# A slot-attention and mixture-of-experts kernel: all engines' calls in another planned order up to the first tile of expert work

## The chip, the core and the metric

The kernel runs on one NeuronCore of one Trainium2 chip. The time is the device time of one execution in microseconds (us), the median of three runs. All arithmetic is in fp32. The names of the engines are those of the profile: PE is TensorE's matmul and PEld its weight load, DVE is VectorE, ACT is ScalarE, POOL is GpSimd, SP is SyncE, which here issues transfers only.

## The reference, cut to what matters

The input x has 2 batches of 1024 tokens with 256 features. Each token is refined by three rounds of attention over a small context (154 rows a batch) and by a small MLP; then each token goes to 8 of 32 experts, beside one shared expert.

```python
k, v = x_in @ wk + bk, x_in @ wv + bv              # x_in: normalised context
slots = q_mu + exp(q_logsig) * layernorm(x)        # one slot per token
for _ in range(3):
    q = ln(slots) @ wq + bq
    attn = softmax(k q^T / scale, over the slots) + 1e-8   # so a softmax spans all 1024 tokens
    slots = (attn / attn.sum(over context)) v @ wu + bu + slots
    slots = gelu(ln(slots) @ w1 + b1) @ w2 + b2 + slots
    slots = ln(slots + cond)
x = x + slots
h = layernorm(x)
scores = sigmoid(h @ gate_w.T)                     # 32 experts, 8 chosen in 4 of 8 groups
combine = 2.5 * scores[chosen] / sum
out = x + sum_e combine_e * (silu(h gate_e) * (h up_e)) down_e + shared(h)
```

## The kernel before, in words

The 2048 tokens are four blocks of 512: blocks 0 and 1 are the first batch, 2 and 3 the second. The program has two parts.

**The front.** Each block passes three rounds. In one round r, a block i goes through these calls, each of which is a helper function on one engine with the same name in the engines' programs: `square` (ACT, L1394) and `from_squares` (POOL, L545 to L540) give the variance and rstd of the slots, `normalise` (ACT, L1402) writes them, `transpose_slots` (PE, L1649) turns them, `evacuate` (ACT, L1409) copies them out of PSUM, and `logits` (PE, L1663) multiplies with the keys. `maxima` (DVE, L771) and `exponent_bias` (DVE, L781, L787), one for both blocks of a batch, `exponent` (ACT, L1419) and `scale_values` (DVE, L794 to L803) make the softmax. `attend` (PE L1678, DVE L811 to L765) comes in two halves a block; the second half on PE waits until DVE has read the banks of the first. Then square, from_squares, normalise, transpose and evacuate again, `hidden` (PE L1689), `gelu` (ACT L1429), `project_back` (PE L1702), `condition` (POOL L568 or DVE L822, which adds the condition row to 512 tokens), `residual` (DVE L831), `slot_moments` (DVE L733 to L739), `from_moments` (POOL L536) and `norm_slots` (DVE L743, L749). A softmax needs both blocks of its batch, so a batch's blocks go in step; the two batches are independent of each other.

After round 2 a block is routed: `add_tokens` (DVE L840 and moments), `from_tokens` (POOL L559), `normalise` into tokrow (ACT L1402), `transpose_block`, `copy_tokens` (ACT L1436), `gate_logits` (PE L1714), `score_tokens` (ACT L1440), `choose` (DVE L855 to L891: the 8 experts), `weigh` (DVE L896 to L909), `rank` (PE L1723 to L1729: at which place of its expert each token goes) and `find_places` (DVE L920 to L930). POOL's `dispatch` (L609) then scatters the block's 512 token rows to DRAM with 32 indirect DMAs, two in each of 16 steps. It waits for placed and weighed of its block. Beside this run the shared expert (`shared_gate_up` PE L1781 and L1787, `shared_silu` ACT L1446, `shared_product` DVE L1020, `shared_down` PE L1798, `add_shared` DVE L1028) and the tables of which expert each tile has (`count_runs` PE L1744, `tabulate_runs`, `tabulate_steps`, `tabulate_tiles` DVE, `sum_runs` and `spread_runs` PE), in three phases. The first phase needs blocks 0 and 1, the last one all blocks.

**The tiles.** 159 tiles of 128 token rows follow. SP fetches a tile, PE turns it (L1886), multiplies with its expert's weights (L2027), turns the activation (L2040) and multiplies down (L2047); ACT writes the weighted result (`copy_out`, L1477). POOL scatters 153 of these results to DRAM (`scatter`, L704), each when its result is there. After dispatch step 12 of block 2, POOL issues one scatter after each dispatch step, until the dispatches of blocks 2 and 3 are all out. At the end SP fetches the results in token order, DVE adds them, and SP stores them. `turn_act(0)`, the first L2040, waits until all four blocks' shared results are added.

**What sets the order.** Each engine works through its queue strictly in program order and waits at semaphores. The order of the front is a plain list of calls written out by hand or by a planner in each engine's program, and this list is all that the change touches. A call that waits holds back everything behind it on its engine, on POOL the dispatches too. From the first tile on the order is that of loops.

## Time and profile before

| | us |
|---|---|
| median of 3 runs | 616.68 (615.47 to 618.01) |
| profiled execution, span | 615.6 |
| median less span | 1.1 |
| PE busy | 563.7 (92%) |
| POOL busy | 363.9 (59%) |
| first dispatch starts | 212.26 |
| first turn of an activation (L2040) starts | 336.40 |
| last scatter starts | 590.54 |

The span is from the first to the last instruction on the core; no other time of the profiled execution is given. Issuing an indirect DMA counts as busy on POOL, the 0.3 us between two of them do not, so POOL's 59% understates how full its queue is.

### The profile page before, as it was taken

Reading aid. Unit: us, or ns where it says so; the run is one execution under the profiler, and the core shown is the slowest. Engines: PE = TensorE matmul, PEld = TensorE weight load, DVE = VectorE, ACT = ScalarE, POOL = GpSimd, SP = SyncE. Lnnn points to the kernel's source line nnn. Section 1 sums busy time; section 2 is a strip of 40 time slices with the busy share of each in tenths; the row PEclk is TensorE's granted clock in tenths of the full one; section 3 lists DMA queues with packets and bytes.
Section 4 is the critical chain, followed back from the end, with each engine's and each line's share of the span. In section 5 each row is a group of like instructions: output and inputs, shape, how many; then the busy total and the mean of one; then the engine's idle time right before and its main releaser. Section 6 shows DMA issues by size and latency. Waiting matters only on the chain.

```text
span 615.6 us, 11543 instructions
## 1 busy us (share of the span) xinstructions
PE 563.7 (92%) x2669; PEld 419.9 (68%) x2669; DVE 411.4 (67%) x1587; ACT 372.2 (60%) x993; POOL 363.9 (59%) x414
## 2 busy tenths in 40 slices
PE   3989989889998898698998999999999999999995
PEld 2656557655766455455656888888888888888774
DVE  6965675986768987648776444445444444698778
ACT  1858888768776755552611666566566666676660
POOL 4334233622143377886777777777777777777730
PEclk9979999999999799899799999999999999999998
DMA  7999300000000023239364999876666667999956
GB/s 259 394 397 380 120 0 2 0 1 0 2 0 1 14 94 118 97 118 341 119 223 179 314 315 338 284 224 205 202 207 201 210 199 216 353 412 397 413 184 244
DMA packets 62063, 119.69 MB, mean 194 GB/s; under 512 B 8667, under 2 KB 45583, under 8 KB 59951
## 3 DMA queue, kind: packets, MB, share of 16 engines
q1 hardware_dynamic: 48079, 77.63, 37.5%
q0 software_dynamic: 13488, 41.04, 17.7%
q8 instruction: 25, 0.41, 0.3%
q10 hardware_dynamic: 432, 0.29, 0.2%
q14 instruction: 39, 0.32, 0.2%
HBM read 61.29 MB, written 57.64 MB: 193 GB/s over the span
## 4 chain that ended last, share of the span: by engine, by line
PE 70%; DVE 10%; POOL 6%; ACT 6%; DMA 5%; issue 3%; SPq 0%; DVEq 0%; POOLq 0%; ACTq 0%
PE ps L2027 20%; PE ps L2047 10%; PE ps L1689 6%; PE ps L1663 6%; PE ps L1678 5%; PE ps L1886 5%; PE ps L1702 5%; POOL xrows L609 4%; DMA hat<-yrows 3%; PE ps L2040 3%; PE ps L1649 2%; PE ps L1781 2%; PE ps L1787 2%; DVE tokrow L749 2%; DMA xs<-in_x 1%
## 5 line engine op out<-in xcount | busy, mean ns | idle before, releaser
L2027 PE MATMUL ps<-arena,mats 128*128 x636 | 164.2, 381 | 0.3 <-issue 0.3
L609 POOL DMA_INDIRECT xrows<-tokrow,place_of x128 | 125.8, 983 | 42.9 <-issue 37.2
L1274 DVE TENSOR_TENSOR mats<-ps,mats 128x128 f32<-128x128 f32 x159 | 46.3, 291 | 104.1 <-ACT mats L1460 99.8
L2027 PEld LDWEIGHTS ps<-arena,mats 128*128 128x128 f32 x636 | 108.5, 190 | 9.3 <-issue 0.8
L2047 PE MATMUL ps<-arena,mats 128*128 x318 | 95.7, 383 | 1.0 <-DVE mats L1281 1.0
L1460 ACT ACTIVATE mats<-ps 128x128 f32<-128x128 f32 x159 | 44.1, 277 | 57.0 <-PE ps L2027 57.0
L1453 ACT COPY mats<-ps 128x256 f32<-128x256 f32 x159 | 57.9, 364 | 11.8 <-PE ps L1886 11.8
L1402 ACT ACTIVATE hat<-tokrow,shift,rstd 128x256 f32<-128x256 f32 x96 | 49.7, 590 | 14.1 <-POOL shift L540 14.1
L1394 ACT ACTIVATE hat<-tokrow,total 128x256 f32<-128x256 f32 x96 | 47.5, 499 | 17.0 <-DVE tokrow L814 10.3
L2047 PEld LDWEIGHTS ps<-arena,mats 128*128 128x128 f32 x318 | 48.0, 191 | 13.5 <-issue 1.9
L545 POOL TENSOR_SCALAR var_eps<-variance 128x4 f32<-128x4 f32 x24 | 6.4, 266 | 83.5 <-ACT hat L1394 83.2
L704 POOL DMA_INDIRECT yrows<-hatT,mats x48 | 46.4, 967 | 14.6 <-issue 10.4
L1689 PE MATMUL ps<-hatT,arena 128*128 128x512 f32 x96 | 48.6, 654 | 4.4 <-ACT hatT L1409 4.4
L1702 PE MATMUL ps<-mats,hat 128*128 128x256 f32 x192 | 44.4, 384 | 4.5 <-ACT hat L1429 4.5
L1663 PE MATMUL ps<-hatT,arena 128*128 128x512 f32 x96 | 44.8, 615 | 2.1 <-ACT hatT L1409 2.1
L2040 PE MATMUL ps<-ident,mats 128*128 128x128 f32 x159 | 43.6, 274 | 2.7 <-DVE mats L1274 2.5
L704 POOL DMA_INDIRECT yrows<-tokrow,mats x38 | 38.5, 1013 | 11.6 <-issue 9.4
L1702 PEld LDWEIGHTS ps<-mats,hat 128*128 128x128 f32 x192 | 35.6, 190 | 13.7 <-ACT hat L1429 4.8
L1678 PE MATMUL ps<-arena 128*128 128x257 f32 x192 | 44.3, 384 | 0.1
L1678 PEld LDWEIGHTS ps<-arena 128*128 128x128 f32 x192 | 36.1, 192 | 6.8 <-DVE arena L803 1.2
L1689 PEld LDWEIGHTS ps<-hatT,arena 128*128 128x128 f32 x96 | 19.8, 211 | 27.1 <-issue 21.2
L536 POOL TENSOR_TENSOR rstd<-var_eps,minus_half 128x4 f32<-128x4 f32 x16 | 18.6, 1165 | 29.1 <-DVE var_eps L739 29.0
(239 smaller groups left out, 1136.4 us busy)
## 6 DMA issues: line engine op xcount, KB each, us to landing
hat<-xrows SPq DMA_DIRECT2D x81, 160.0 KB
rows<-xrows SPq DMA_DIRECT2D x78, 160.0 KB
arena<-in_experts SPq DMA_DIRECT2D x4, 1920.0 KB, 18.9
xrows<-padrow SPq DMA_DIRECT2D x32, 160.0 KB
hat<-yrows SPq DMA_DIRECT2D x5, 1024.0 KB, 9.0
tokrow<-yrows SPq DMA_DIRECT2D x5, 1024.0 KB, 9.6
hatT<-yrows SPq DMA_DIRECT2D x5, 1024.0 KB, 9.3
xrows<-padrow SPq DMA_DIRECT2D x1, 4960.0 KB
```

Source lines behind the costliest of these rows:

```text
L609: gp.indirect_dma_start(out=xrows[:, :], out_offset=bass.IndirectOffsetOnAxis(ap=place_of[:, g, k:k + 1], axis=0), in_=tokrow[:, g, :], in ...
L704: gp.indirect_dma_start(out=yrows[:, :], out_offset=bass.IndirectOffsetOnAxis(ap=scatter_to[:, n:n + 1], axis=0), in_=ybuf[y_place(n)], in ...
L1394: it = ac.activation(hat[:, g, :], slots[:, g, :], ACT.Square, bias=total[:, g:g + 1], scale=-float(D), accum_out=variance[:, g:g + 1])
L1402: ac.activation(into[:, g, :], source[:, g, :], ACT.Identity, bias=shift[:, g:g + 1], scale=rstd[:, g:g + 1]).then_inc(normed[i // Q], 1)
L1453: ac.copy(turned_row[u], bank(4 + u)[:, 0:D]).then_inc(row_copied, 1)
L1663: mm = te.matmul(bank(banks_of(i)[h]), kq[:, dc, j * NH:j * NH + P], hatT[b][:, dc, span_of(i)], start=dc == 0, stop=dc == DC - 1)
L1678: mm = te.matmul(bank(banks_of(i)[k])[:, 0:D + 1], attn[b][:, h, t * P:(t + 1) * P], vscaled[b][:, h, 0:D + 1], start=h == 0, stop=h == 1)
L1689: mm = te.matmul(bank(banks_of(i)[fc]), w1g[:, dc, fc * P:(fc + 1) * P], hatT[b][:, dc, span_of(i)], start=dc == 0, stop=dc == DC - 1)
L1702: mm = te.matmul(bank(banks_of(i)[k])[:, t * D:(t + 1) * D], gel[i][:, fc, s:s + P], mat("w2", fc), start=fc == 0, stop=fc == DC - 1)
L2027: mm = te.matmul(bank(6 + u)[:, 0:2 * I], turned_row[u][:, dc * P:(dc + 1) * P], arena[:, dc * D:(E - 1) * WCOL + (dc + 1) * D][:, bass.ds ...
L2040: te.transpose(bank(u)[:, 0:I], act[u], ident[:, :]).then_inc(act_turned, 1)
L2047: te.matmul(bank(2 + u)[:, 0:D], actT[u], arena[:, 2 * D:(E - 1) * WCOL + 3 * D][:, bass.ds(at, D)], start=True, stop=True).then_inc(down_ ...
```

## The change

Four lists of calls have another order: those of POOL, DVE, ACT and PE, from the start to the first tile. No call is added, removed or altered, and SP's program is the same. On the whole the calls of the second batch's attention stand later among those of the first batch; `constants` and `run_constants` move, and in the last stage the shared expert's calls and the counts stand elsewhere. The core of the diff, PE first, then DVE and POOL:

```diff
             attend(0, 2, 1)
+            transpose_slots(3, 2)
             attend(1, 2, 1)
+            logits(3, 1)
+            transpose_slots(0, 5)
+            transpose_slots(1, 5)
+            hidden(0, 2)
             attend(2, 1, 0)
-            attend(3, 1, 0)
-            attend(2, 1, 1)
-            transpose_slots(0, 5)
-            attend(3, 1, 1)
-            hidden(0, 2)
-            transpose_slots(1, 5)
             project_back(0, 2)
             hidden(1, 2)
+            project_back(1, 2)
+            attend(2, 1, 1)
+            attend(3, 1, 0)
             transpose_slots(2, 3)
-            project_back(1, 2)
+            attend(3, 1, 1)
+            transpose_block(0, 2 * ROUNDS, slots)
+            gate_logits(0)
             hidden(2, 1)
             project_back(2, 1)
+            rank(0)
             transpose_slots(3, 3)
-            transpose_block(0, 2 * ROUNDS, slots)
-            gate_logits(0)
             hidden(3, 1)
-            rank(0)
...
+            spread_runs(0)
             project_back(2, 2)
-            shared_gate_up(1, 0)
             hidden(3, 2)
...
             sum_runs(1)
-            shared_gate_up(3, 1)
             spread_runs(1)
             count_runs(2)
+            shared_gate_up(3, 1)
+            sum_runs(2)
             shared_down(3)
...
             slot_moments(1)
+            attend(2, 1, 1)
             add_tokens(0)
-            residual(2, 1)
-            slot_moments(2)
-            norm_slots(2, 1)
+            attend(3, 1, 0)
+            norm_slots(1, 2)
+            attend(3, 1, 1)
+            add_tokens(1)
             choose(0)
             weigh(0)
             find_places(0)
...
             from_tokens(0)
             from_moments(1, 4)
-            from_moments(2, 3)
-            from_squares(2, 4)
+            from_squares(3, 3)
+            from_tokens(1)
             dispatch(0, 0)
             dispatch(0, 1)
+            from_moments(2, 3)
             dispatch(0, 2)
-            from_tokens(1)
             dispatch(0, 3)
+            from_squares(2, 4)
             from_moments(3, 3)
```

On PE, from the first batch's last project_back (the first L1702; mats is w2, hat is gelu's output) to rank(0) (L1723, whose input mats is the table of chosen experts). Before:

```order
L1702 MATMUL ps<-mats,hat 128x256 x8
L1689 MATMUL ps<-hatT,arena 128x512 x4
L1702 MATMUL ps<-mats,hat 128x256 x8
L1649 MATMUL ps<-ident,hat 128x128 x8
L1649 MATMUL ps<-ident,tokrow 128x128 x8
L1714 MATMUL ps<-gwT,hatT 128x32 x8
L1689 MATMUL ps<-hatT,arena 128x512 x4
L1723 MATMUL ps<-mats,routing 128x128
```

and in the changed program, the same stretch:

```order
L1702 MATMUL ps<-mats,hat 128x256 x8
L1678 MATMUL ps<-arena 128x257 x8
L1649 MATMUL ps<-ident,hat 128x128 x8
L1678 MATMUL ps<-arena 128x257 x4
L1649 MATMUL ps<-ident,tokrow 128x128 x8
L1714 MATMUL ps<-gwT,hatT 128x32 x8
L1689 MATMUL ps<-hatT,arena 128x512 x4
L1702 MATMUL ps<-mats,hat 128x256 x8
L1723 MATMUL ps<-mats,routing 128x128
```

Three halves of the second batch's attention (L1678) have come between the last project_back of the first batch and the gate, and the block that hidden and project_back (L1689, L1702) serve behind the gate is now block 2, both of them ahead of rank(0).

On POOL, from the last from_tokens ahead of the dispatches on (L559 is from_tokens, L609 the dispatches, L536 from_moments, L545 to L540 from_squares). Before:

```order
L559 TENSOR_TENSOR rstd<-var_eps,minus_half 128x4
L540 TENSOR_TENSOR shift<-neg_mean,rstd 128x4
L536 TENSOR_TENSOR rstd<-var_eps,minus_half 128x4 x2
L545 TENSOR_SCALAR var_eps<-variance 128x4
L548 TENSOR_TENSOR rstd<-var_eps,minus_half 128x4
L540 TENSOR_TENSOR shift<-neg_mean,rstd 128x4
L609 DMA xrows<-tokrow,place_of 73600x320 x6
L559 TENSOR_TENSOR rstd<-var_eps,minus_half 128x4
L540 TENSOR_TENSOR shift<-neg_mean,rstd 128x4
L609 DMA xrows<-tokrow,place_of 73600x320 x2
```

and in the changed program:

```order
L559 TENSOR_TENSOR rstd<-var_eps,minus_half 128x4
L540 TENSOR_TENSOR shift<-neg_mean,rstd 128x4
L609 DMA xrows<-tokrow,place_of 73600x320 x4
L536 TENSOR_TENSOR rstd<-var_eps,minus_half 128x4
L609 DMA xrows<-tokrow,place_of 73600x320 x4
L545 TENSOR_SCALAR var_eps<-variance 128x4
L548 TENSOR_TENSOR rstd<-var_eps,minus_half 128x4
L540 TENSOR_TENSOR shift<-neg_mean,rstd 128x4
L536 TENSOR_TENSOR rstd<-var_eps,minus_half 128x4
L609 DMA xrows<-tokrow,place_of 73600x320 x4
```

from_tokens(1) has moved ahead of the first dispatch, and from_moments(2, 3) and from_squares(2, 4), which stood ahead of it, now stand between the dispatches.

## Rows read from the trace of the kernel before

**Rows 1.** The chain that ended last, its end: start us, us, what

```profile
590.54 4.44 DMA yrows<-tokrow,mats
...
595.03 4.97 DMA hat<-yrows
```

**Rows 2.** POOL's timeline: start us, us, what, [idle before <-releaser]

```profile
212.26 1.21 POOL L609 DMA_INDIRECT xrows<-tokrow,place_of  x1 [5.40 <-DVE place_of L929]
...
221.36 1.04 POOL L559 TENSOR_TENSOR rstd<-var_eps,minus_half 128x4 f32<-128x4 f32 x1 [1.25 <-DVE var_eps L739]
...
283.72 1.04 POOL L536 TENSOR_TENSOR rstd<-var_eps,minus_half 128x4 f32<-128x4 f32 x1 [1.47 <-DVE var_eps L739]
...
288.44 1.20 POOL L559 TENSOR_TENSOR rstd<-var_eps,minus_half 128x4 f32<-128x4 f32 x1 [1.18 <-DVE var_eps L739]
...
311.94 0.96 POOL L609 DMA_INDIRECT xrows<-tokrow,place_of  x1 [0.30 <-issue]
```

**Rows 3.** The page's groups, the dispatches: count, busy us, mean ns, idle before

```profile
L609 POOL DMA_INDIRECT xrows<-tokrow,place_of x128 | 125.8, 983 | 42.9 <-issue 37.2
```

**Rows 4.** ACT's timeline, its write of the last scattered result

```profile
589.43 0.47 ACT L1477 ACTIVATE tokrow<-ps,mats 128x256 f32<-128x256 f32 x1
```

**Rows 5.** PE's timeline from the first batch's last attention on

```profile
158.02 12.30 PE L1678 MATMUL ps<-arena 128*128 128x257 f32 x56
...
172.77 3.60 PE L1689 MATMUL ps<-hatT,arena 128*128 128x512 f32 x8
...
177.14 3.72 PE L1702 MATMUL ps<-mats,hat 128*128 128x256 f32 x16
...
203.30 6.47 PE L1689 MATMUL ps<-hatT,arena 128*128 128x512 f32 x8 [1.33 <-ACT hatT L1409]
```

**Rows 6.** POOL's condition and DVE's exponent_bias beside it, and one by itself

```profile
59.18 4.66 POOL L568 TENSOR_TENSOR tokrow<-tokrow,rows 128x1024 f32<-128x1024 f32 x2
...
61.13 2.73 DVE L781 SCALAR_TENSOR_TENSOR shifted<-rowmax,qk_bias 77x1 f32<-77x1 f32 x2
...
95.37 0.35 DVE L781 SCALAR_TENSOR_TENSOR shifted<-rowmax,qk_bias 77x1 f32<-77x1 f32 x2
```

**Rows 7.** DVE's timeline, norm_slots(0, 2) to weigh(0)

```profile
184.76 1.66 DVE L743 SCALAR_TENSOR_TENSOR tokrow<-tokrow,mv,rows 128x256 f32<-128x256 f32 x4
...
187.97 0.68 DVE L831 TENSOR_TENSOR tokrow<-ps,tokrow 128x512 f32<-128x512 f32 x1
...
191.56 1.22 DVE L840 TENSOR_TENSOR xs<-xs,tokrow 128x1024 f32<-128x1024 f32 x1
...
195.11 0.69 DVE L831 TENSOR_TENSOR tokrow<-ps,tokrow 128x512 f32<-128x512 f32 x1 [0.20 <-PE ps L1702]
...
202.90 0.29 DVE L855 TENSOR_TENSOR mats<-mats,gbias 128x128 f32<-128x128 f32 x1
...
208.19 0.28 DVE L896 TENSOR_TENSOR mats<-mats 128x128 f32<-128x128 f32 x1
```

**Rows 8.** Two stretches: us, busy of PE, PEld, DVE, ACT, POOL; PEclk, DMA, GB/s

```profile
202.10:208.90 6.80, 5.60 (x7) 2.50 (x8) 6.22 (x45) 5.11 (x15) 1.41 (x3) 0.50 0.00 0
256.70:263.50 6.80, 5.79 (x11) 2.52 (x11) 2.42 (x3) 5.09 (x10) 5.78 (x7) 0.50 0.27 98
```

**Rows 9.** PE's timeline: logits(3, 2), transpose_slots(2, 5), last project_back, first L2040

```profile
234.30 3.70 PE L1663 MATMUL ps<-hatT,arena 128*128 128x512 f32 x8 [1.05 <-ACT hatT L1409]
...
255.86 2.17 PE L1649 MATMUL ps<-ident,hat 128*128 128x128 f32 x8 [3.63 <-ACT hat L1402]
...
277.06 3.72 PE L1702 MATMUL ps<-mats,hat 128*128 128x256 f32 x16 [0.78 <-ACT hat L1429]
...
336.40 0.33 PE L2040 MATMUL ps<-ident,mats 128*128 128x128 f32 x1 [0.96 <-DVE mats L1274]
```

**Rows 10.** DVE's timeline, the row behind choose(2), and tabulate_runs(2)

```profile
302.58 0.69 DVE L1020 TENSOR_TENSOR hat<-ps,hat 128x512 f32<-128x512 f32 x1
...
326.17 0.19 DVE L955 SCALAR_TENSOR_TENSOR pad_at<-ps,first_row 128x32 int32<-128x32 f32 x1 [2.02 <-PE ps L1744]
```

More of the change, by code:

```diff
@@ L625, in gpsimd_program @@
             condition(0, 0)
+            constants()
             condition(1, 0)
@@ L1130, in vector_program @@
             slot_moments(1)
+            norm_slots(1, 0)
             attend(2, 0, 0)
-            norm_slots(1, 0)
+            maxima(0, 1)
+            attend(3, 0, 0)
             attend(2, 0, 1)
-            attend(3, 0, 0)
-            maxima(0, 1)
+            attend(3, 0, 1)
             maxima(1, 1)
             exponent_bias(0, 1)
-            attend(3, 0, 1)
             scale_values(0, 1)
@@ L1184, in vector_program @@
             find_places(0)
-            run_constants()
-            norm_slots(1, 2)
+            condition(2, 1)
+            residual(2, 1)
+            slot_moments(2)
             condition(3, 1)
-            add_tokens(1)
+            norm_slots(2, 1)
             residual(3, 1)
@@ L1191, in vector_program @@
             norm_slots(3, 1)
-            shared_product(0, 0)
             choose(1)
@@ L1196, in vector_program @@
             exponent_bias(1, 2)
-            shared_product(0, 1)
+            shared_product(0, 0)
+            scale_values(1, 2)
             find_places(1)
-            scale_values(1, 2)
+            weigh(1)
+            attend(3, 2, 0)
+            attend(2, 2, 0)
+            attend(2, 2, 1)
+            attend(3, 2, 1)
             tabulate_runs(0)
-            attend(2, 2, 0)
             tabulate_steps(0)
-            attend(3, 2, 0)
-            attend(2, 2, 1)
-            tabulate_tiles(0)
-            attend(3, 2, 1)
-            weigh(1)
             condition(2, 2)
-            add_shared(0)
             residual(2, 2)
             slot_moments(2)
-            shared_product(1, 0)
+            tabulate_tiles(0)
             condition(3, 2)
+            shared_product(0, 1)
             norm_slots(2, 2)
@@ L1216, in vector_program @@
             slot_moments(3)
+            add_tokens(2)
+            add_shared(0)
+            shared_product(1, 0)
             shared_product(1, 1)
-            add_tokens(2)
             norm_slots(3, 2)
             add_tokens(3)
+            choose(2)
             add_shared(1)
-            choose(2)
             shared_product(2, 0)
```

188 lines of the change are left out of this document (90 added, 98 removed).

## The prediction, made before the changed kernel ran

> **What bounds the kernel now.** I read the end of the chain of waits first. The last scatter's transfer lands at 594.98, one fetch of 4.97 us and the last sums follow [rows 1]. So the end hangs on the last scatter, which is issued at 590.54. Then POOL's timeline, backwards: from the first dispatch at 212.26 [rows 2] it issues 128 dispatches and 153 scatters, and an issue costs 0.98 us and some 0.29 us between two (37.2 us over 126) [rows 3], so about 1.27 us. 281 of them are 356 us of the 378 us between 212.26 and 590.54; the other 22 us are small operations of the front that stand between the dispatches, and short waits. POOL's queue is thus full to the end. But the tiles finish beside it: ACT has written the last scattered result at 589.90 [rows 4], 0.64 us before its scatter, so only some 0.3 us of slack are left beyond the usual gap. So there are two clocks that have to be moved together: POOL's first dispatch with what stands between the dispatches, and PE's first tile. The later of the two sets the end. The last of the tables that the tiles read need the last round of the second batch, so the first tile hangs on the second batch's chain; the first dispatch hangs on the first batch's.
>
> **The stretch 150 to 215.** Before, PE does seven halves of attention in one piece, 12.30 us, 1.76 us each [rows 5]; the last of them are the second batch's, and they fill the time in which DVE, ACT and POOL carry the first batch from its attention to hidden(0, 2) at 172.77. The changed order puts these halves later and hides nothing in their place. I follow it with the durations of before.
> - Up to the first batch's last attention the shifts cancel within 1.5 us: the softmax of batch 0 no longer queues behind logits(2, 1) and (3, 1), and attend(0, 2, 0) starts 1.4 us earlier, after an idle PE of some 3 us. Hidden(0, 2) starts at about 171.8, 1.0 earlier.
> - Now gelu(0, 2) stands on ACT behind exponent(2, 1) and (3, 1), and those wait for logits(3, 1) (ends 168.6), maxima(3, 1) and exponent_bias(1, 1) (at 169.4). Just then POOL adds condition(0, 2) and (1, 2). Beside such a pair exponent_bias took 2.73 us and ended with POOL; alone it takes 0.35 [rows 6]. Held, the two exponents end at 176.7, gelu(0, 2) at 179.3, and project_back(0, 2) starts at 179.7 in place of 177.14 [rows 5]: 2.5 us late. Not held, it is 0.4 late.
> - By 3.60 and 3.72 us for hidden and project_back [rows 5], project_back(1, 2) then ends at 191.4 (held case). DVE: residual and moments to 194.2, attend(2, 1, 1) 1.4, add_tokens(0) 3.4 (191.56 to 195.11, less 0.2 of wait), attend(3, 1, 0) 1.4, norm_slots(1, 2) 3.3 (184.76 to 187.97) [rows 7], attend(3, 1, 1) 1.4, add_tokens(1) 3.4: choose(0) can start at 207.9, in place of 202.90.
> - PE has little in 191 to 206: three halves, of which the last waits for DVE until 200, two transposes, and the gate. Before, a thinner stretch of this kind, 197 to 203, ended with the clock granted at 0.50 for 6.8 us [rows 8], and hidden(3, 1) took 6.47 instead of 3.60 [rows 5], 2.9 us more. I take the same for hidden(2, 1): 206.2 to 212.7.
> - rank(0) stands behind it and project_back(2, 1): gelu, 3.72 us, rank 1.0, ends at 218.1. Choose(0) ends at 213.2 (5.29 us, 202.90 to 208.19) [rows 7] and weigh at 215.4, so it is rank that decides. With find_places 1.5 the first dispatch starts at 220.0: 7.7 late; at full clock 5.0.
>
> **From there to the end.** Two sums.
> - POOL: from the first dispatch to dispatch(2, 0) before 99.7 us (212.26 to 311.94) [rows 2]. Out goes from_tokens(1) with its 1.25 us wait, 2.7; in come from_moments(2, 3) 1.3 and from_squares(2, 4) 1.85; the waits of 1.47 and 1.18 [rows 2] go, since DVE and PE are ahead of the later queue there; two waits of 0.4 us come for from_squares(2, 5) and (3, 5). Together 2.2 us less. So dispatch(2, 0) is at 7.7 - 2.2 = 5.5 late. From it on the queue is the same.
> - PE: rank(0), hidden(3, 1) and project_back(3, 1) come in a row from 218.1, project_back(3, 1) also behind transpose_block(1) and ends at 230.5 (10 us late). Residual, moments, norm_slots(3, 1) (behind from_moments(3, 3), which waits for POOL's dispatches) and the same again for from_squares(3, 4) bring logits(3, 2) to 245.0, 10.7 after the 234.30 of before [rows 9]. From there 5 us come back: hidden(3, 2) follows project_back(2, 2) without the shared_gate_up(1, 0) of 3.6 us between, and I charge no half clock there (before, 6.8 us at 0.50 [rows 8] added some 2.4 to hidden(2, 2)); 0.8 is lost otherwise. The last project_back starts at 282.5, 5.4 after 277.06 [rows 9]. Choose(2) is then 7.8 late at 310.3 (302.5 before [rows 10]), since shared_product(1, 1) now waits in front of norm_slots(3, 2) (2.4). In the tables 1.4 comes back: count_runs(2) no longer stands behind shared_gate_up(3, 1), so DVE's wait of 2.02 [rows 10] goes, but shared_product(3, 1) and add_shared(3) still hold the end. First turned activation: 336.40 + 7.8 - 1.4 = 342.8, 6.4 late.
>
> The end follows the later: 6.4 less the 0.3 us of slack that results had to scatters, 6.1. Its lower bound is with both doubtful terms out: 2.1 (exponent_bias not held) and 2.9 (clock not dropped), 1.1. Its upper bound is a second drop of the clock in the thin stretch around 250 to 256, where before a drop followed at 256.7 [rows 8]: two halves at half speed, 3 us, so 9.1. Whether exponent_bias is held turns on tenths of a microsecond, so I count half of it: 6.1 - 1.1 = 5.0. The span would be 620.6, and with the 1.1 us by which the median stands above it, 621.7.
>
> Two rules of the Trainium skill bear on these two terms. "SBUF — State Buffer", section "SBUF: two separate sides", says that VectorE operations with two SBUF inputs and GpSimd exclude each other from a shared port pair for a whole instruction; the trace agrees with 2.73 us against 0.35 [rows 6]. By it alone the hold would count in full, and the time would be 622.8. "TensorE: Matmul & The Clock Gate", Part 1, says that an idle array falls to half rate and that activity releases it; the trace shows the same at 202.1 [rows 8]. It speaks against any order that leaves PE thin, and by it the half clock would count in full, as I have it.
>
> **Rivals.**
> 1. A wash. The doubtful terms fall away and the front's last stage gives more than I count: POOL's 2.2 us and the tables' 1.4 us are certain by order, and if rank(0) ends by 212 and choose(2) at its old place, both clocks shift by -1.4: 615.3. For it: a walk over 150 calls drifts, and mine has the early part even. Against: DVE alone puts choose(0) 3 to 5 us later. Range 614 to 619.
> 2. Faster. The place is the second batch's last round: before, PE waits 3.63 us ahead of transpose_slots(2, 5) [rows 9] and then runs at 0.50 until 263.5 [rows 8], 6 us together. If that hole closes and the first dispatch is not late, PE's first tile comes 6 us earlier, and POOL decides with its 2.2 us and what the first dispatch gains; with 2 us gained there, 4 us in all: 612.7. It needs the first dispatch before 213, from which point on it decides. Against: three of DVE's calls and two of PE's are newly ahead of it.
> 3. Much slower. POOL waits in its queue for the second batch (from_squares(2, 4), from_moments(3, 3), from_squares(3, 4), each with dispatches behind it), since that batch is 10 us late while the dispatches are 7.7: every microsecond of such a wait is one at the end. Three waits of 1.5 us and the second drop of the clock give 5.0 + 4.5 + 3 = 12: 629.
> 4. That nothing moves, because the end is set by something the order doesn't touch: excluded, since both clocks begin in the reordered part.
>
> **How the numbers follow.** My forecast, 617.8 to 625.8 (1.1 to 9.1 late), has 0.55; the wash 0.25; faster 0.14; much slower 0.06. 0.5% is 3.1 us, about what a measurement of this kernel can tell from no change: faster is below 613.6, slower above 619.8. Of my forecast a sixth lies below 619.8. Slower: 0.46 + 0.06, about 0.53; same: 0.09 + 0.22, 0.31; faster: 0.14 and a little of the wash, 0.16. The range for 8 in 10 is 613.0 to 627.0; the forecast's own is 617.8 to 625.8.
>
> **What would show it.** Of the changed kernel: POOL's first dispatch at 217 to 220 and dispatch(2, 0) 2 us less late than it; PE idle for 10 us or more between 186 and 206 and a clock of 0.50 behind that; rank(0), PE's first L1723, as late as the dispatch behind it; exponent_bias at about 170 with 2 us or more; logits(3, 2) 10 us late; the first L2040 at 341 to 343; the last scatter at 595 to 597. I am wrong if the first dispatch is before 214, or if DVE reaches choose(0) by 204.

## The result: 3.8% slower, 23 us where 5 were forecast, and the profile after

The changed kernel takes 639.4 us (median of 4 runs, 638.13 to 643.0) against 616.08 of the kernel before beside it (4 runs, 614.92 to 618.01): a ratio of 1.038, 95% interval 1.035 to 1.041. The sign was right and the size was not: 639.4 lies far above my range.

The end of the chain of waits of the changed kernel (start us, us, what), for [rows 1]:

```profile
615.68 2.77 DMA yrows<-tokrow,mats
...
618.50 4.88 DMA hat<-yrows
```

The last scatter is 25.1 us later than before. POOL's timeline, first dispatch and last scatter (in brackets the idle time before and what ended it), for [rows 2]:

```profile
224.59 2.06 POOL L609 DMA_INDIRECT xrows<-tokrow,place_of  x1 [9.26 <-DVE place_of L929]
...
615.68 1.32 POOL L704 DMA_INDIRECT yrows<-tokrow,mats  x1 [0.61 <-ACT tokrow L1477]
```

The first dispatch is 12.3 us late, but POOL's queue no longer decides: its last scatter waits 0.61 us for ACT. The tiles decide, and PE's first turned activation is at 363.02 in place of 336.40 [rows 9], 26.6 late; from it to the end of the span take 276.0 us in place of 279.2. So the question is where PE's 26.6 us arose. PE's account up to its first turned activation, of the kernel before (span of time, busy of PE, PEld, DVE, ACT, POOL with counts, mean granted clock, DMA share, GB/s):

```profile
0.00:336.40 336.40, 293.95 (x1205) 194.34 (x1205) 249.15 (x1013) 205.31 (x478) 168.84 (x217) 0.96 0.36 129
```

and of the changed kernel:

```profile
0.00:363.02 363.02, 304.16 (x1205) 202.57 (x1205) 248.30 (x1013) 202.97 (x476) 173.73 (x222) 0.93 0.34 122
```

The same 1205 matmul records take 304.16 us in place of 293.95: 10.2 us more. I put them down to the clock, which is at 0.50, the lower of its two levels, for 47.6 us of this time in place of 27.2: work that fills 20.4 us at half clock would take 10.2 less at full. Idle PE is 58.9 us in place of 42.5, 16.4 more. These two sum to the 26.6.

Where they lie, by calls on PE (before, after, late by): turn_context 8.89, 13.79, 4.9; attend(0, 2, 0) 158.02, 159.05, 1.0; project_back(0, 2) 177.14, 182.81, 5.7; gate_logits(0) 200.03, 210.46, 10.4; rank(0) 209.61, 221.93, 12.3; logits(3, 2) 234.30, 253.13, 18.8; last project_back 277.06, 293.27, 16.2; gate_logits(2) 293.64, 309.73, 16.1; rank(2) 303.18, 326.25, 23.1; first turned activation 26.6. Four places made them, shown here from the timelines of the changed kernel.

The top. DVE before, then DVE and PE of the changed kernel:

```profile
8.33 1.38 DVE L1039 TENSOR_SCALAR arena<-arena,mv,rstd 77x256 f32<-77x256 f32 x4 [1.16 <-POOL rstd L531]
...
11.24 1.41 DVE L733 BATCH_NORM_STATS2 stat<-xs 128x6 f32<-128x256 f32 x4 [4.30 <-DMA xs<-in_x]
...
13.24 1.37 DVE L1039 TENSOR_SCALAR arena<-arena,mv,rstd 77x256 f32<-77x256 f32 x4
...
13.79 1.78 PE L1807 MATMUL ps<-ident,arena 77*128 77x77 f32 x8 [13.79 <-DVE arena L1039]
```

norm_context (L1039) stands behind token_moments(0), which waits for the transfer of x until 11.24. Before, it ran at 8.33, beside that wait.

The hold, around project_back(0, 2) (POOL, DVE, ACT, PE), for [rows 5, 6]:

```profile
171.42 4.66 POOL L568 TENSOR_TENSOR tokrow<-tokrow,rows 128x1024 f32<-128x1024 f32 x2 [0.40 <-ACT hat L1402]
...
171.98 4.12 DVE L781 SCALAR_TENSOR_TENSOR shifted<-rowmax,qk_bias 77x1 f32<-77x1 f32 x2
...
179.14 0.16 DVE L794 TENSOR_TENSOR rowtotal<-rowsum 77x2 f32<-77x2 f32 x1 [2.79 <-ACT arena L1419]
...
176.26 0.68 ACT L1419 ACTIVATE arena<-ps,expbias 77x512 f32<-77x512 f32 x1 [1.99 <-DVE expbias L787]
...
180.19 2.83 PE L1678 MATMUL ps<-arena 128*128 128x257 f32 x8 [2.18 <-DVE arena L803]
182.81 4.52 PE L1702 MATMUL ps<-mats,hat 128*128 128x256 f32 x16
```

The two exponent_bias operations take 4.12 us beside POOL's conditions, which run from 171.42 to 176.08: the hold of my forecast, at 171.98 where I had it at 169.4. Of these 2.6 us 2.4 come from before: attend(0, 2, 0) is 1.0 late where I had it 1.4 early. What the walk lacked is scale_values(1, 1) behind the exponents: PE's attend(2, 1, 0) waits 2.18 us for it, ahead of project_back(0, 2), and then both run at a low clock, 2.83 and 4.52 us in place of 1.9 and 3.6.

From the first batch's end to the second's logits (PE, DVE, ACT), for [rows 5, 7, 9]:

```profile
202.63 2.17 PE L1649 MATMUL ps<-ident,hat 128*128 128x128 f32 x8 [3.90 <-ACT hat L1402]
204.59 3.63 PE L1678 MATMUL ps<-arena 128*128 128x257 f32 x8
...
212.51 5.09 PE L1689 MATMUL ps<-hatT,arena 128*128 128x512 f32 x8
...
213.90 0.29 DVE L855 TENSOR_TENSOR mats<-mats,gbias 128x128 f32<-128x128 f32 x1 [1.01 <-ACT mats L1440]
...
240.38 0.28 ACT L1440 ACTIVATE mats<-ps 128x128 f32<-128x128 f32 x1 [4.19 <-PE ps L1714]
...
245.58 5.63 PE L1663 MATMUL ps<-hatT,arena 128*128 128x512 f32 x8 [2.22 <-ACT hatT L1409]
...
253.13 3.70 PE L1663 MATMUL ps<-hatT,arena 128*128 128x512 f32 x8 [1.05 <-ACT hatT L1409]
```

transpose_slots(2, 3) waits 3.90 us, attend(3, 1, 1) behind it takes 3.63 at the low clock, and gate_logits(0) is late behind both; choose(0) waits for it. Later ACT's score_tokens(1) (L1440) stands 4.19 us for gate_logits(1), which PE runs behind shared_gate_up(0, 0), with normalise(2, 4) and square(3, 4) in its queue; logits(2, 2) waits and then takes 5.63 us.

The last stage (POOL, DVE, then PE), for [rows 2, 9, 10]:

```profile
332.19 0.96 POOL L609 DMA_INDIRECT xrows<-tokrow,place_of  x1 [4.41 <-issue]
...
327.80 0.29 DVE L920 TENSOR_TENSOR mats<-ps,first_row 128x128 f32<-128x128 f32 x1 [4.97 <-PE ps L1729]
...
331.38 0.69 DVE L1020 TENSOR_TENSOR hat<-ps,hat 128x512 f32<-128x512 f32 x1
331.99 0.28 DVE L855 TENSOR_TENSOR mats<-mats,gbias 128x128 f32<-128x128 f32 x1
...
349.08 0.19 DVE L955 SCALAR_TENSOR_TENSOR pad_at<-ps,first_row 128x32 int32<-128x32 f32 x1 [1.74 <-PE ps L1744]
...
312.10 6.49 PE L1798 MATMUL ps<-shared,hat 128*128 128x256 f32 x16
...
326.25 0.47 PE L1723 MATMUL ps<-mats,routing 128*128 128x128 f32 x2
...
348.91 3.44 PE L1781 MATMUL ps<-hatT,shared 128*128 128x512 f32 x4
...
354.92 3.72 PE L1798 MATMUL ps<-shared,hat 128*128 128x256 f32 x16 [0.76 <-DVE hat L1020]
...
363.02 0.27 PE L2040 MATMUL ps<-ident,mats 128*128 128x128 f32 x1
```

find_places(2) (L920) waits 4.97 us for rank(2), which stands behind gate_logits(3); choose(3) (331.99) is 23.8 late, against 308.18 before. shared_down(1) takes 6.49 us where 3.7 is usual, and shared_gate_up(3, 1) 3.44 + 1.88 where twice 1.88 is. The first row is dispatch(2, 0): it needs weigh(2), which DVE has done at 331.42, behind find_places(2).

### The profile page after: what moved, and what is told of

It is laid out like the page before. It is cut to its first block, busy times and chain, and to the rows that moved or that the text cites. A ratio compares the mean times of both kernels' runs of the same rounds, so it can differ in the third digit from the quotient of the medians.

```text
span 639.0 us, 11542 instructions
## 1 busy us (share of the span) xinstructions
PE 574.0 (90%) x2669; PEld 428.2 (67%) x2669; DVE 410.3 (64%) x1587; ACT 370.4 (58%) x992; POOL 364.5 (57%) x414
## 4 chain that ended last, share of the span: by engine, by line
PE 70%; ACT 13%; DVE 11%; DMA 3%; POOL 2%; issue 2%; SPq 0%; DVEq 0%; POOLq 0%; ACTq 0%
PE ps L2027 21%; PE ps L2047 10%; PE ps L1886 5%; PE ps L1702 5%; PE ps L1678 5%; PE ps L1689 4%; PE ps L1663 4%; ACT hat L1394 4%; PE ps L1798 3%; PE ps L2040 3%; ACT hat L1402 3%; PE ps L1649 2%; ACT arena L1419 2%; PE ps L1781 2%; ACT hatT L1409 1%
## 5 line engine op out<-in xcount | busy, mean ns | idle before, releaser
L609 POOL DMA_INDIRECT xrows<-tokrow,place_of x128 | 127.7, 997 | 51.2 <-issue 41.6
L545 POOL TENSOR_SCALAR var_eps<-variance 128x4 f32<-128x4 f32 x24 | 5.0, 210 | 109.1 <-ACT hat L1394 108.9
L1394 ACT ACTIVATE hat<-tokrow,total 128x256 f32<-128x256 f32 x96 | 47.6, 499 | 27.5 <-DVE tokrow L814 21.3
L1678 PE MATMUL ps<-arena 128*128 128x257 f32 x192 | 51.0, 421 | 12.1 <-DVE arena L803 9.4
L2047 PEld LDWEIGHTS ps<-arena,mats 128*128 128x128 f32 x318 | 48.0, 191 | 13.7 <-issue 2.1
L1402 ACT ACTIVATE hat<-tokrow,shift,rstd 128x256 f32<-128x256 f32 x96 | 49.4, 591 | 11.3 <-POOL shift L540 11.2
L1678 PEld LDWEIGHTS ps<-arena 128*128 128x128 f32 x192 | 39.4, 211 | 22.4 <-DVE arena L803 12.5
L1663 PE MATMUL ps<-hatT,arena 128*128 128x512 f32 x96 | 45.5, 622 | 5.4 <-ACT hatT L1409 5.4
L1702 PE MATMUL ps<-mats,hat 128*128 128x256 f32 x192 | 45.2, 389 | 4.7 <-ACT hat L1429 4.7
L1689 PE MATMUL ps<-hatT,arena 128*128 128x512 f32 x96 | 45.1, 614 | 3.8 <-ACT hatT L1409 3.8
L1702 PEld LDWEIGHTS ps<-mats,hat 128*128 128x128 f32 x192 | 36.5, 194 | 14.2 <-ACT hat L1429 6.4
L2040 PE MATMUL ps<-ident,mats 128*128 128x128 f32 x159 | 43.6, 274 | 0.6 <-DVE mats L1274 0.6
L536 POOL TENSOR_TENSOR rstd<-var_eps,minus_half 128x4 f32<-128x4 f32 x16 | 19.0, 1186 | 31.7 <-DVE var_eps L739 31.6
L1663 PEld LDWEIGHTS ps<-hatT,arena 128*128 128x128 f32 x96 | 18.3, 198 | 26.9 <-issue 18.8
```

The lines of the kernel that those rows point to most:

```text
L609: gp.indirect_dma_start(out=xrows[:, :], out_offset=bass.IndirectOffsetOnAxis(ap=place_of[:, g, k:k + 1], axis=0), in_=tokrow[:, g, :], in ...
L1394: it = ac.activation(hat[:, g, :], slots[:, g, :], ACT.Square, bias=total[:, g:g + 1], scale=-float(D), accum_out=variance[:, g:g + 1])
L1402: ac.activation(into[:, g, :], source[:, g, :], ACT.Identity, bias=shift[:, g:g + 1], scale=rstd[:, g:g + 1]).then_inc(normed[i // Q], 1)
L1663: mm = te.matmul(bank(banks_of(i)[h]), kq[:, dc, j * NH:j * NH + P], hatT[b][:, dc, span_of(i)], start=dc == 0, stop=dc == DC - 1)
L1678: mm = te.matmul(bank(banks_of(i)[k])[:, 0:D + 1], attn[b][:, h, t * P:(t + 1) * P], vscaled[b][:, h, 0:D + 1], start=h == 0, stop=h == 1)
L1689: mm = te.matmul(bank(banks_of(i)[fc]), w1g[:, dc, fc * P:(fc + 1) * P], hatT[b][:, dc, span_of(i)], start=dc == 0, stop=dc == DC - 1)
```

## Experiments

All ran against the kernel before on the same chip. Line numbers in their rows are mostly one higher (L1650 for L1649), for a line that was added above. "Late at the first tile" is the first turned activation against 336.40.

Traces are one execution each, and shifts in them have noise of their own. Five traces (the changed kernel, a_rank2, a_tables, a_last2b, a_oldlast) have the same order up to gate_logits(2) and reach it at 309.7, 307.7, 312.1, 309.7 and 306.8. A shift of 1 or 2 us late in the front is therefore not shown by one trace.

### Which stretch

Four mixtures: one order until a time, and for what is left the order of the other kernel. No call is changed.

```
early_only   changed to 152 us | before
mid_only     before to 146 us  | changed to 224.5 us | before
late_only    before to 211 us  | changed
last_only    before to 285 us  | changed
```

> The changed order up to the second batch's second-round logits (what the changed kernel starts before 152 us), the old order from there on. Theory A (each stretch of the front loses its own time, and the losses add at the first tile): the shift at attend(0, 2, 0) is 1.0 us in the changed kernel's trace, so the end is 0 to 1.5 us late, 616 to 618. Theory B (the early order leaves the second batch further behind, and that is what the later stretches pay for): logits(3, 1) is late here too, and with it the end, 621 or more.

> The old order until 146 us, the changed one for what the changed kernel starts between there and its first dispatch (224.5 us), the old order again after it. Theory A: first dispatch 11 to 12 us late (12.3 in the changed kernel, less 1.0 of the early part), and since POOL's queue is full to the end, the end is 10 to 12 late: 626 to 629. Theory B (the first dispatch is absorbed and only the later order costs): under 620. Theory C (the whole loss comes out of this stretch): 635 or more.

> The old order until 211 us, just before the first dispatch, and the changed order from there on. Theory A: 3.9 us lost between the first dispatch and the last project_back (16.2 less 12.3) and 10.4 between there and the first turned activation (26.6 less 16.2): the first turned activation 10 to 14 us late, the end 8 to 12 late, 624 to 629. My forecast's own account of this stretch, which I now call the rival: 1.4 us come back in the tables and up to 5 us on the way to the last project_back: 612 to 616.

> The old order until 285 us, behind the last project_back, and the changed order from there: gate_logits(3) ahead of rank(2), shared_down(1) behind gate_logits(2), shared_gate_up(3, 1) behind count_runs(2), shared_silu(2, 0) ahead of normalise(3, 6). Theory A: first turned activation 7 to 10 us late, the end 6 to 9 late, 622 to 626. Rival (what the changed kernel loses here is only that its first batch's leftovers, shared_down(0) and shared_gate_up(1, 0), were pushed into this stretch; the order itself costs little): 616 to 619.

Measured: 628.08 (ratio 1.024, 1.017 to 1.031), 630.88 (1.027, 1.022 to 1.033), 632.3 (1.032, 1.024 to 1.040) and 627.36 (1.022, 1.017 to 1.027); late at the first tile 11.2, 16.2, 17.9 and 10.7 us. Early, middle and late alone add up to 45 us where the change as a whole has 26.6, so they can't be read as its parts: three of them make waits at the seam, which neither whole order has. In early_only (PE, then ACT):

```profile
161.05 2.17 PE L1650 MATMUL ps<-ident,hat 128*128 128x128 f32 x8 [7.07 <-ACT hat L1403]
...
160.39 2.08 ACT L1403 ACTIVATE hat<-tokrow,shift,rstd 128x256 f32<-128x256 f32 x4 [1.68 <-POOL shift L540]
```

ACT has square(3, 2) and normalise(3, 2) behind exponent(0, 2) (in the changed order they stand behind exponent(1, 2) too), but PE keeps logits(3, 1) ahead of the first batch's attention, as before: PE stands 7.07 us. In mid_only POOL:

```profile
220.70 1.17 POOL L536 TENSOR_TENSOR rstd<-var_eps,minus_half 128x4 f32<-128x4 f32 x1 [12.34 <-DVE var_eps L740]
...
227.27 1.21 POOL L609 DMA_INDIRECT xrows<-tokrow,place_of  x1 [0.70 <-issue]
```

from_moments(2, 3) of the second batch stands in front of the first dispatch, 12.34 us. And in late_only:

```profile
219.56 1.91 POOL L559 TENSOR_TENSOR rstd<-var_eps,minus_half 128x4 f32<-128x4 f32 x1 [13.01 <-DVE var_eps L740]
...
222.45 1.21 POOL L609 DMA_INDIRECT xrows<-tokrow,place_of  x1 [0.70 <-issue]
```

from_tokens(1) stands there for 13.01 us, since DVE has add_tokens(1) behind choose(0). What is clean in them: mid_only reaches rank(0) 3.8 us late and its own early part ran 1.3 ahead, so the middle alone costs 5.2 up to rank(0). That is near the 5.0 of my forecast with hidden(2, 1) at full clock, and hidden(2, 1) does take 3.68 us here; but the clock was at 0.50 from 194.4 to 201.4, over other calls, so the agreement is in part luck. And last_only, with all before it as in the kernel before (1.7 ahead at 277), loses 12.3 us in the last stage alone.

### The first call

```
 DVE, b_context: kernel before      DVE, a_context: changed kernel
-norm_context()                    +norm_context()
 token_moments(0)                   token_moments(0)
+norm_context()                    -norm_context()
```

> The kernel before with one swap on DVE: token_moments(0), which waits for the transfer of x, ahead of norm_context. Theory A (the front is a chain from its first call, so a late start is late everywhere): turn_context 4.7 us late and the first dispatch and the first turned activation 3.5 to 5 late, the end 619 to 621. Theory B (the early front has slack, as my forecast took it when it called the early part even): the shift is gone by the first dispatch, 615 to 617.

> The changed kernel with norm_context ahead of token_moments(0) again and nothing else. Theory A: the end 4 to 5 us earlier than the changed kernel, 634 to 636. Theory B: the same as the changed kernel, 638 to 640.

b_context: 619.79 against 615.62, ratio 1.0068 (1.0045 to 1.0091), 4.2 us. a_context: 635.68, ratio 1.032 (1.025 to 1.039), 3.7 less than the changed kernel's 639.4. b_context is clear of noise: one swap of two neighbours at 8 us is seen at the end, theory A. a_context has the sign and size of theory A, but its interval reaches 1.039 and so takes in the changed kernel's 1.038; its trace has attend(0, 2, 0) 4.3 us earlier than the changed kernel and the first tile 2.1. Of b_context's 5.0 us at turn_context 2.7 are left from 73 us on, 2.9 at the first tile and 3.2 in the profiled span.

### The last stage

```
 PE, a_rank2 (and a_last2, a_last2b)   DVE, a_last2, a_last2b only
 shared_gate_up(2, 0)                  -shared_product(2, 1)
+rank(2)                                choose(3)
 transpose_block(3, 6)                 +shared_product(2, 1)
 gate_logits(3)
-rank(2)
 PE, a_tables, also a_oldlast          DVE, a_tables, also a_oldlast
 sum_runs(1)                            tabulate_runs(2)
+shared_gate_up(3, 1)                  +tabulate_steps(2)
 spread_runs(1)                        +tabulate_tiles(2)
 count_runs(2)                          add_shared(2)
-shared_gate_up(3, 1)                  -tabulate_steps(2)
 ...                                    add_shared(3)
                                       -tabulate_tiles(2)
```

a_oldlast has all of these and normalise(3, 6) ahead of shared_silu(2, 0) on ACT. b_last2 is the reverse of a_last2b's two moves, in the kernel before.

> The changed kernel with rank(2) on PE ahead of transpose_block(3) and gate_logits(3) again. Theory A (the placing of rank(2) alone holds up find_places(2), choose(3) and the tables): find_places(2) 4 us earlier, first turned activation 3 to 4 earlier, 635.5 to 637. Rival (gate_logits(3), behind shared_silu(2, 0) on ACT, holds choose(3) at the same time anyway): within 1 us of the changed kernel.

> The changed kernel with the last tables in the old order: shared_gate_up(3, 1) ahead of spread_runs(1) on PE, tabulate_steps(2) and tabulate_tiles(2) ahead of add_shared on DVE. Theory A (in the changed order sum_runs(2) waits for shared_gate_up(3, 1) and the tables for the shared expert's leftovers, some 5 us in the trace, 351.8 to 359.3 in place of the 3.5 that before takes): first turned activation 3 to 5 earlier, 635 to 637. My forecast's account (1.4 us came back by that change): 640 to 641.5.

a_rank2: 641.75, ratio 1.042 (1.039 to 1.046), 2.4 more than the changed kernel (the intervals overlap), not less. a_tables: 646.24, 1.050 (1.046 to 1.053), 6.8 more. Both against theory A. DVE of a_rank2:

```profile
319.99 0.28 DVE L921 TENSOR_TENSOR mats<-ps,first_row 128x128 f32<-128x128 f32 x1
...
330.78 0.69 DVE L1021 TENSOR_TENSOR hat<-ps,hat 128x512 f32<-128x512 f32 x1 [7.17 <-PE ps L1788]
331.39 0.28 DVE L856 TENSOR_TENSOR mats<-mats,gbias 128x128 f32<-128x128 f32 x1
```

find_places(2) does come 7.8 us earlier (2.0 of it were there at gate_logits(2)), and choose(3) starts at 331.39 as ever: shared_product(2, 1), ahead of it, waits 7.17 us for shared_gate_up(2, 1), which runs at half clock. One wait had hidden the other. In a_tables the front was already 2.3 us later at gate_logits(2), in the same order, and its clock was at 0.50 from 354.6 to 358.0 and 361.4 to 368.2, over the first tiles.

> The changed kernel with rank(2) on PE ahead of transpose_block(3) and shared_product(2, 1) on DVE behind choose(3), as before. Theory A (two waits in one another's shadow): choose(3) 5 us earlier than the changed kernel's 332.0, the first turned activation 4 to 6 earlier, the end 634 to 636. Rival (PE's work, at a low clock, is the bound of the last stage): within 2 us of the changed kernel, 637.5 to 641.

> The changed kernel with the whole old order from rank(2) on: besides the two calls, normalise(3, 6) ahead of shared_silu(2, 0) on ACT and the tables and shared expert's leftovers as before. Theory A: from gate_logits(2) to the first turned activation 42.8 us as before in place of 53.3, plus the 3.7 of shared_down(1), which the changed order leaves to this stretch: 6 to 7 us earlier, 632 to 634. Rival (a_tables went the other way, 6.8 us late, so the old tables cost here): no better than a_last2b, 635 to 640.

> The kernel before with rank(2) behind gate_logits(3) on PE and shared_product(2, 1) ahead of choose(3) on DVE. Theory A: find_places(2) waits for gate_logits(3), 306.4 in place of 304.6, and choose(3) for shared_silu(2, 1) and so for shared_gate_up(2, 1), which ends at 310 to 312: choose(3) 3 to 4 us later, the first turned activation too, the end 618 to 620. Rival (the last stage of the kernel before has room, since POOL is full): under 616.5.

a_last2b: 638.43, ratio 1.038 (1.034 to 1.042), no different from the changed kernel: the rival. DVE and PE:

```profile
327.55 0.29 DVE L856 TENSOR_TENSOR mats<-mats,gbias 128x128 f32<-128x128 f32 x1 [0.62 <-ACT mats L1441]
...
336.45 0.49 PE L1724 MATMUL ps<-mats,routing 128*128 128x128 f32 x2
```

choose(3) comes 4.4 us earlier, but rank(3) only 1.0, because it now stands behind PE's shared_gate_up(3, 0) and count_runs(1), with no wait ahead of it. In the changed kernel it had waited 2.03 us. a_oldlast: 636.05, 1.034 (1.028 to 1.041), 3.4 less, which the intervals don't tell apart; from gate_logits(2) to the first tile it takes 47.6 us where the changed kernel takes 53.3 and the kernel before 42.8. So in this pair of traces the order from rank(2) on is worth 5.7 us of the 10.5, when all of it is taken back together (a_five against a_four, below, gives 2.3). b_last2: 621.2, 1.012 (1.009 to 1.015), 6.3 us. Its waits, on DVE and then PE:

```profile
306.80 0.29 DVE L921 TENSOR_TENSOR mats<-ps,first_row 128x128 f32<-128x128 f32 x1 [4.48 <-PE ps L1730]
...
316.42 0.49 PE L1724 MATMUL ps<-mats,routing 128*128 128x128 f32 x2 [1.84 <-DVE block_sum L892]
...
318.70 4.66 PE L1799 MATMUL ps<-shared,hat 128*128 128x256 f32 x16
```

find_places(2) waits 4.48, choose(3) is 4.0 later against the same early part; that was theory A. But the first tile is 7.0 later by the same measure (5.8 against 336.40, with an early part 1.15 ahead): rank(3) waits 1.84, and two stretches at 0.50 (317.3 to 320.7, 330.9 to 334.3) follow that the kernel before does not have; shared_down(2) takes 4.66 in place of 3.70. PE is busy for 297.96 up to the first tile, 4.0 more than before. From gate_logits(2) to the first tile PE is idle for 2.9 us more and busy for 3.9 more, with 13.6 us at 0.50 in place of 6.8. Waits cost themselves and then the clock.

### The middle

```
 DVE, a_cond                        PE, a_gate1               PE, a_fill
 exponent_bias(1, 1)                +gate_logits(1)           +14 extra matmuls
+condition(0, 2)                     shared_gate_up(0, 0)      transpose_slots(2, 3)
+condition(1, 2)                    -gate_logits(1)            ...
 scale_values(1, 1)                                           +8 extra matmuls
(and both out of POOL's list)                                  logits(2, 2)
```

> The changed kernel with extra matmuls on PE, whose results nobody reads, where PE waits anyway: 14 of 128x256 ahead of transpose_slots(2, 3) (idle 3.90 us there) and 8 ahead of logits(2, 2) (idle 2.22 us). Theory A (a thin PE loses its clock, and the lost clock is part of the delay): the stretch at 0.50 from 201.7 to 208.5 goes, rank(0) comes 3 to 4 us earlier, the end 3 to 5 earlier, 635 to 637. Rival (the half clock lies beside waits for ACT and DVE and costs nothing): within 1 us of the changed kernel, or later by what the fillers delay.

> The changed kernel with condition(0, 2) and condition(1, 2) on DVE, between exponent_bias(1, 1) and scale_values(1, 1), in place of POOL. Theory A (POOL's condition holds exponent_bias(1, 1), 4.4 us from start to end in the changed kernel against 0.6 to 0.8 by itself): exponent(2, 1) 3.5 us earlier, project_back(0, 2) 2.5 to 4 earlier, the end 2 to 4 earlier, 635.5 to 637.5. Rival (DVE pays with 2.4 us for what it saves, or the softmax is not what project_back(0, 2) waits for): within 1 us of the changed kernel.

> The changed kernel with gate_logits(1) on PE ahead of shared_gate_up(0, 0). Theory A (ACT's score_tokens(1) waits behind that call from 234.9 to 239 and holds normalise(2, 4), square(3, 4) and both blocks' logits): logits(3, 2) 2 to 3.5 us earlier, the end 2 to 3 earlier, 636.5 to 637.5. Rival (maxima(2, 2) waits for DVE's choose(1) anyway, so nothing moves): within 1 us.

> The changed kernel with two calls of the last stage back at their old places: rank(2) on PE ahead of transpose_block(3), and shared_product(2, 1) on DVE behind choose(3). With the first alone find_places(2) came at 320.0 in place of 327.8, but choose(3) stood behind shared_product(2, 1) until 331.4. Theory A (two waits in one another's shadow; both must go): choose(3) at 325 to 327 in place of 332.0, first turned activation 4 to 6 us earlier, the end 634 to 636. Rival (the last stage is a plain sum of PE's work and not of waits): within 2 us of the changed kernel.

These four shared a chip on which every kernel, the one before too (722.01 us), took some 100 us more, all of it behind 250 us, so their times (732.08, 731.83, 735.8 and 734.38; ratios 1.016, 1.015, 1.020 and 1.021, each give or take 0.01) tell nothing here; their traces up to 250 us lie over those of the other runs. a_cond, DVE and PE:

```profile
170.86 0.35 DVE L780 SCALAR_TENSOR_TENSOR shifted<-rowmax,qk_bias 77x1 f32<-77x1 f32 x2
...
176.97 2.00 PE L1679 MATMUL ps<-arena 128*128 128x257 f32 x8
178.80 3.62 PE L1703 MATMUL ps<-mats,hat 128*128 128x256 f32 x16
```

The hold is gone: 0.35 us in place of 4.12, attend(2, 1, 0) waits for nothing, and project_back(0, 2) is 1.7 late where the changed kernel is 5.7; 1.1 of the difference was there at 147 us, 2.9 are the hold's. Theory A, up to here; for the end there is no time from a chip like the others. From attend(0, 2, 0) to project_back(0, 2) it is 20.9 us here and in both later kernels without the hold (a_four, a_five), 23.6 to 24.6 in the nine traces of the changed order with it, and 23.0 in mid_only, where the clock stayed up: 2.1 by the hold itself, my forecast's figure, and the rest with the clock. a_gate1: score_tokens(1) waits 0.76 us in place of 4.19, but then normalise(2, 4) waits for POOL:

```profile
240.24 2.08 ACT L1403 ACTIVATE hat<-tokrow,shift,rstd 128x256 f32<-128x256 f32 x4 [2.12 <-POOL shift L540]
```

From rank(0) to logits(3, 2) it loses 5.0 us in place of 6.5: between the theories, 1.5 gained (by the traces alone). a_fill: the stretch at 0.50 from 201.7 went, another of 3.4 us came at 210.2, and rank(0) was 10.3 late in place of 12.3, 1.0 of it from before the fillers; the other 1.0 is less than the same order varies by without fillers (under "The clock"). I had sized the fillers at 0.23 us each and they take 0.44, so they delayed what they should have helped.

### All together

a_four is a_context, a_cond, a_gate1 and a_last2b in one kernel; a_five has the last stage of a_oldlast in place of a_last2b's.

> The changed kernel with four things undone together: norm_context first, condition(0, 2) and condition(1, 2) taken from POOL to DVE, gate_logits(1) ahead of shared_gate_up(0, 0), and rank(2) with shared_product(2, 1) as before. Theory A (the losses add): 3.7 + 2.5 + 1.5 + 5 = 12.7 us earlier, 625 to 628. Rival (they hide one another, the slowest of several chains decides): 631 to 635.

> The changed kernel with norm_context first, condition(0, 2) and condition(1, 2) on DVE, gate_logits(1) ahead of shared_gate_up(0, 0), and the whole old order from rank(2) on. Theory A (the losses add): last project_back 7.2 us late as in the kernel with four things undone, 4.9 more up to the first turned activation as in the kernel with the old last stage, 12 in all; the end 10 to 12 above the kernel before where a_four was 11.8: 624 to 627, hardly better than a_four. Rival (with less waiting the clock stays up as well, and the last stage is worth its full 5.7): 619 to 623.

a_four: 626.66, ratio 1.019 (1.015 to 1.022), 12.7 less than the changed kernel: the sum, by luck. Its parts are others than I wrote, and those of its trace (of the slowest of its four runs, 631.47) come to 10.1 at the first tile: the trace has it 7.2 late at the last project_back, 9.1 earlier than the changed kernel (4.7 for the start, 2.9 for the hold and 1.5 for gate_logits(1) make 9.1, closer than the noise of such traces allows one to tell), and gives back 1.0 in the last stage, as a_last2b alone. a_five: 625.7, 1.016 (1.012 to 1.020), 11.5 us above the kernel before: theory A, hardly better than a_four. 13.9 us are left at the first tile, 6.7 up to the last project_back and 7.1 behind it. Neither version beats the kernel before.

### The clock

In the kernel before, work that nobody reads is put into PE's waits ahead of its three drops of the clock.

```
+3 matmuls ahead of project_back(2, 1), 4 of gate_logits(0), 5 of hidden(3, 1),
+13 of transpose_slots(2, 5), 8 of transpose_block(2, 6), 4 of gate_logits(2)
```

> The kernel before with extra matmuls on PE, whose results nobody reads, where PE waits anyway: 3, 4 and 5 of 128x256 ahead of project_back(2, 1), gate_logits(0) and hidden(3, 1), 13 ahead of transpose_slots(2, 5), 8 and 4 ahead of transpose_block(2) and gate_logits(2). Theory A (the waits bring the clock down): no stretch at 0.50 between 195 and 302 us, hidden(3, 1) 3.6 to 3.8 us in place of 6.47, the first dispatch 1.0 to 1.4 earlier, the first turned activation 2.5 to 5 earlier, and since POOL is full from the first dispatch, the end 1.0 to 1.7 earlier, a ratio of 0.997 to 0.998. Rival (the clock falls whatever PE does there): the stretches stay, and the end is the same or up to 1 us later.

b_fill: 619.8, ratio 1.007 (1.004 to 1.010), 5.6 us later, not earlier. PE:

```profile
204.87 3.60 PE L1690 MATMUL ps<-hatT,arena 128*128 128x512 f32 x8
...
209.17 0.46 PE L1724 MATMUL ps<-mats,routing 128*128 128x128 f32 x2 [0.70 <-DVE block_sum L892]
...
254.49 5.77 PE L1894 MATMUL ps<-mats 128*128 128x256 f32 x26
```

On the clock theory A holds where there are fillers: no stretch at 0.50 begins at 202, 257 or 294, and hidden(3, 1) takes 3.60 us in place of 6.47 [rows 5] and hidden(2, 2) 3.70 in place of 5.94. It fails for the stretch 195 to 302 as a whole: new ones of 3.4 us come at 212.8 and 229.9, the first right behind a wait of 2.3 us that has no filler, the second behind one of 1.05, and one of 6.8 comes at 305.0. On the time it fails, by my sizing: 13 fillers take 5.77 us (x26, two records to a call), where the wait was 3.63, so PE is 4.2 late at transpose_slots(2, 5), and the first tile 3.7. rank(0) gains 0.9 on attend(0, 2, 0) (0.4 against 209.61), after a wait of 0.70 for choose(0), and the first dispatch, at 212.70, gains nothing.

What the clock costs by itself the traces show without fillers. Eight traces have the changed order from attend(0, 2, 0) to rank(0), and this stretch takes 60.6 us with 6.8 of them at 0.50 (a_oldlast), 60.8 with 10.2 (a_rank2), 62.9 with 13.7 (the changed kernel, a_last2, a_last2b) and 64.2 to 64.4 with 17.1 (a_context, a_gate1, a_tables); PE's busy time goes from 50.6 to 54.6, its idle time stays between 9.8 and 9.9. In the order of before the stretch is 51.6 to 51.7 in four traces (the kernel before, b_context, b_last2, last_only), each with 6.8 at 0.50 and 3.3 idle. So the changed order adds 6.5 us of idle time to this stretch, and PE's longer busy time 2.3 to 6.3 more.

## Why the prediction was wrong

The forecast at the first tile was 7.7 + 3.0 - 5.3 + 2.4 - 1.4 = 6.4 us late; measured, by the same stretches, it is 12.3 + 6.5 - 2.6 - 0.1 + 10.5 = 26.6. So 9.4 us were missed behind the last project_back, 4.6 up to rank(0), 3.5 and 2.7 between. The steps that failed, with what the runs show:

- **"Mine has the early part even."** Failed, and worth 4.2 us at the end (b_context; a_context has 3.7, within its noise), and 4.7 at attend(0, 2, 0), where the changed kernel is 1.0 late and mid_only 3.6 early; the swap alone gives 4.3 of it (a_context). I compared calls by their durations and did not read what DVE waits for at the very top. A transfer's landing was moved in front of the first link of the chain.
- **The stretch 150 to 215, 7.7 late, or 5.0 at full clock.** Right in mechanism: the hold came as forecast and is worth 2.9 (a_cond), and the stretch by itself costs 5.2 with hidden(2, 1) at full clock (mid_only). In the changed kernel 12.3 less the start's 4.7 leaves 7.6, with the clock down, though by other calls than hidden(2, 1) alone (5.09 of the 6.47 I took). That it falls on my 7.7 is luck: the same order takes 60.6 to 64.4 us for this stretch. My times for DVE's calls also add up to choose(0) at 208.5, not 207.9, which decided nothing. I halved the hold for doubt, and it came in full, as the rule of the Trainium skill has it ("SBUF — State Buffer", section "SBUF: two separate sides"): the trace agrees with 4.12 us against 0.35.
- **"PE ... 5 us come back" up to the last project_back, and logits(3, 2) 10.7 late.** It was 18.8 late: 12.3 at rank(0), 4.7 of them the start's, and from there on 6.5 in place of my 3.0, with score_tokens(1) (1.5, a_gate1) and logits(2, 2) at half clock among them. Then 2.6 came back, not 5.3.
- **"In the tables 1.4 comes back."** The worst term: from gate_logits(2) to the first tile 10.5 us were lost (last_only: 12.3 by itself). I looked at the wait that the new order removes (2.02 of DVE [rows 10]), which is still 1.74 in the changed kernel (at 349.08), and not at rank(2) behind gate_logits(3), nor at choose(3) behind shared_product(2, 1), two moves worth 6.3 us in the kernel before (b_last2). Taking them back in the changed kernel gained 1.0, within the noise (a_last2b), and of the 10.5 us only 2.3 to 5.7 come back with the whole order from rank(2) on; for the rest the cause stays open, save that shared_down(1), 3.7 us of work at full clock, now stands in this stretch.
- **Both clocks tied, POOL 2.2 less.** POOL lost 7.9 us between its first dispatch and dispatch(2, 0) (12.3 and 20.3 late), with a wait of 4.62 for the second batch ahead of from_squares(2, 5) and one of 4.41 ahead of dispatch(2, 0), which my sum had at its old 0.3. By its own terms that sum also gives 1.4 less, not 2.2 (I left out the two waits of 0.4); PE would have decided by it all the same. PE was later still, so this cost nothing. Of rival 3, much slower at 629, the waits on POOL came, larger than it had them, but they did not decide; what did was PE, on the second batch's chain.
- **The clock as two doubtful terms, 2.9 and 3.** It goes along with the waits all through the front: 10.2 of the 26.6 us are the same work taking longer, with 20.4 us more at 0.50. b_fill shows for three places that the drop goes when the wait ahead is filled; in b_last2 choose(3) 4.0 us later became 7.0 at the first tile.

Four things taken back together win back 12.7 of the 23 us (a_four). Open: what makes the 13.9 us that a_five still has at the first tile. Its middle keeps the changed places of the attention halves and of hidden(2, 1), which I did not take apart; shared_down(1) between gate_logits(2) and shared_gate_up(2, 0) is left to its last stage.

## What to carry to other kernels

An order of calls is priced by its waits, each with what stands behind it in the same queue; read first the calls that wait for a transfer, and the order near the end, where nothing is left to hide in. Two moves can hide one another: undoing one then shows nothing (a_rank2), so undo by stretches as well as singly, and cut a mixture of two orders only where both have the same calls done on all engines. On TensorE, count a new wait for more than itself while the stretch around it is thin.

## What the runs showed of the hardware that I had not expected

- A matmul call of 128x256 in float32 is two records and 0.44 us (13 calls, x26, 5.77 us); the count in a row is not the count of calls.
- DVE's operation with two SBUF inputs waits for POOL's tensor operation even where it is tiny: two of 77x1 took 4.12 us beside POOL's 171.42 to 176.08, and 0.35 without it, while the reduction over PSUM at 171.19 took 0.69.
- One chip ran every kernel some 100 us slower behind 250 us, with engines idle while the inputs that the profile names were there. In a_cond DVE's next operation behind rank(3), which had ended at 349.9, waited:

```profile
361.12 0.29 DVE L919 TENSOR_TENSOR mats<-ps,first_row 128x128 f32<-128x128 f32 x1 [11.77 <-remote]
```

11.77 us for what the profile can't name. Ratios of such a chip (1.015 to 1.021) say little on a change that is worth 1.038 elsewhere.
